# Delta stage: another order of the operations inside a steady slot

## The reference

```python
q = silu(dwconv_causal(x @ Wq, conv_q_w, conv_q_b))     # k and v likewise, 4 taps
alpha = sigmoid(x @ Wa + ba); beta = sigmoid(x @ Wb + bb)
def step(S, inp):                                       # 16 heads, DK = DV = 128, 256 steps
    err = einsum('bhvk,bhk->bhv', S, kt) - vt
    S = at * S - bt * err[..., None] * kt[:, :, None, :]
    return S, einsum('bhvk,bhk->bhv', S, qt)
o = scan(step, S0, (q, k * scale, v, alpha, beta))
o = (o - mean(o)) * rsqrt(var(o) + 1e-05) * ln_w + ln_b # per head
o = (o * sigmoid(x @ Wg)).reshape(B, T, H * DV) @ Wo
```

## Time and profile before

| | |
|---|---|
| median of 3 runs | 3179.25 us (3178.41 to 3184.36) |
| the profiled execution, its own time | 3174.32 us |
| its span, first to last instruction | 3172.5 us |
| PE busy | 2712.6 us, 86% |
| DVE busy | 2251.3 us, 71% |
| ACT busy | 2126.5 us, 67% |
| POOL busy | 2001.5 us, 63% |
| mean granted TensorE clock | 0.943 of full |

### The profile page before, as it was taken

The page is one execution under the profiler, slowest core; times in us unless marked ns, Lnnn a source line. Parts: engine busy times, 40 slices in busy tenths (PEclk is TensorE's granted clock), DMA queues, the critical chain, the costliest instruction groups (busy, mean ns, idle before and its releaser), DMA issues.

```text
span 3172.5 us, 65475 instructions
## 1 busy us (share of the span) xinstructions
PE 2712.6 (86%) x21872; PEld 2201.8 (69%) x21872; DVE 2251.3 (71%) x5574; ACT 2126.5 (67%) x4995; POOL 2001.5 (63%) x2171
## 2 busy tenths in 40 slices
PE   6889889646679999999999999999999999976761
PEld 4555555425568888888888888888888888765651
DVE  5777777575546767767767677677677676688877
ACT  4767776324458778777777777777787787754531
POOL 3544554333766878677786776868768777676432
PEclk9999999667889999999999999999999999988976
DMA  2000000014577676776767767677676767633311
GB/s 98 0 0 0 0 0 0 3 56 126 119 205 193 163 201 156 190 195 160 203 149 192 195 162 197 159 189 191 167 182 173 188 178 176 160 87 88 86 29 53
DMA packets 750313, 402.07 MB, mean 127 GB/s; under 512 B 406867, under 2 KB 686163, under 8 KB 749910
## 3 DMA queue, kind: packets, MB, share of 16 engines
q1 hardware_dynamic: 750038, 398.59, 48.6%
HBM read 263.80 MB, written 134.62 MB: 126 GB/s over the span
## 4 chain that ended last, share of the span: by engine, by line
PE 52%; ACT 6%; DVE 5%; POOL 4%; issue 3%; SPq 0%; DMA 0%; DVEq 0%; POOLq 0%; ACTq 0%
PE bank L2041 22%; PE bank L2092 8%; PE bank L2208 7%; PE bank L2072 4%; PE bank L2156 4%; ACT acc L1116 2%; POOL oT L896 2%; ACT shifted L1114 2%; PE bank L2080 2%; PE bank L2198 1%; PE bank L2126 1%; PE bank L2135 1%; PE bank L2114 1%; ACT oT L1191 1%; ACT TT L1171 1%
## 5 line engine op out<-in xcount | busy, mean ns | idle before, releaser
L863 POOL TENSOR_TENSOR acc<-acc,shifted 128x510 f32<-128x510 f32 x384 | 557.4, 1452 | 455.8 <-DVE acc L1637 455.8
L1637 DVE SCALAR_TENSOR_TENSOR acc<-bank,conv_w,acc 128x254 f32<-128x254 f32 (+1 forms) x1536 | 630.6, 472 | 271.3 <-ACT acc L1116 270.9
L2041 PE MATMUL bank<-x_k,w_kq 128*128 128x256 f32 x2048 | 509.5, 399 | 25.1 <-DMA x_k<-xT_scratch 25.1
L1114 ACT ACTIVATE shifted<-bank,conv_w 128x255 f32<-128x255 f32 x768 | 368.0, 479 | 178.6 <-issue 113.6
L2041 PEld LDWEIGHTS bank<-x_k,w_kq 128*128 128x128 f32 x2048 | 388.5, 197 | 90.2 <-issue 15.2
L1116 ACT ACTIVATE acc<-bank,conv_b,conv_w 128x256 f32<-128x256 f32 x768 | 439.9, 573 | 0.0
L776 POOL TENSOR_TENSOR prob<-prob,rinv 128x512 f32<-128x512 f32 x192 | 202.0, 1055 | 265.9 <-DVE rinv L1433 265.7
L880 POOL TENSOR_TENSOR inv<-inv,outer 128x30 f32<-128x30 f32 (+14 forms) x480 | 287.6, 599 | 37.6
L1660 DVE TENSOR_TENSOR LM<-bank,dec 128x512 f32<-128x512 f32 x256 | 167.7, 687 | 155.7 <-PE bank L2072 146.6
L2208 PE MATMUL bank<-w_o,oT 128*128 128x256 f32 x1024 | 247.3, 386 | 24.5 <-POOL oT L896 23.7
L877 POOL TENSOR_TENSOR outer<-inv 128x30 f32<-128x30 f32 (+14 forms) x480 | 242.7, 506 | 35.6 <-DMA inv<-D_scratch 8.0
(11 more groups left out here) (243 smaller groups left out, 5905.5 us busy)
## 6 DMA issues: line engine op xcount, KB each, us to landing
abc<-decay_scratch SPq DMA_DIRECT2D x64, 512.0 KB, 5.3
MTm<-M_scratch SPq DMA_DIRECT2D x128, 256.0 KB, 3.4
kqm<-q_scratch SPq DMA_DIRECT2D x64, 512.0 KB, 4.6
knm<-k_scratch SPq DMA_DIRECT2D x64, 258.0 KB, 3.2
x_k<-xT_scratch SPq DMA_DIRECT2D x64, 256.0 KB, 2.9
q_scratch<-kq SPq DMA_DIRECT2D x128, 128.0 KB, 2.7
q_scratch<-kq SPq DMA_DIRECT2D x64, 256.0 KB, 3.4
D_scratch<-LM SPq DMA_DIRECT2D x256, 64.0 KB, 2.4
```

Source lines behind the costliest of these rows:

```text
L863: pool.tensor_tensor(dst, dst, shifted[:, u % 2, :, 1:], ALU.add).then_inc(Z["sumk" if u < 4 else "sumv"], 1)
L1114: act.activation(shifted[:, u % 2, i % 2, 1:], pj[:, 0:SEQ - 1], ACT.Copy, scale=conv_w[:, kind, bass.ds(head, 1), TAPS - 2:TAPS - 1].rear ...
L1637: dve.scalar_tensor_tensor(out=acc[:, kind, i, t:], in0=pj[:, 0:SEQ - t], scalar=wcol, in1=acc[:, kind, i, t:], op0=ALU.mult, op1=ALU.add) ...
L2041: mm = pe.matmul(dst[:, i * SEQ:(i + 1) * SEQ], w[:, k, head * DK:(head + 1) * DK], x[:, k, :], start=(k == 0), stop=(k == CT - 1))
```

## The change

In a steady slot the calls are put into another order on ACT, DVE and PE, and the shares of the elimination on POOL are dealt out anew. No operation is added, taken away or altered. The diff:

```diff
 PIECES = 4 * BATCH - 4
-SHARE = (2, 4, 2, 1, 1, 4, 2, 1, 1, 4, 2, 0)
+SHARE = (2, 5, 0, 2, 2, 5, 0, 2, 2, 4, 0, 0)
...
# ScalarE
                     tap(2), joined("x"), tap(3), silu(0)
                     if h is not None:
-                        gate(0), state()
+                        state(), gate(0)
                     tap(4), tap(5)
                     if h is not None:
                         gate(1)
                     silu(1)
                     if n is not None:
-                        affine(0), affine(1)
-                    keys(p), silu(2)
+                        affine(0)
+                    keys(p)
+                    if n is not None:
+                        affine(1)
                     if h is not None:
-                        first_out(), from_state()
-                    values(0), values(1)
+                        from_state()
+                    silu(2), values(0)
+                    if h is not None:
+                        first_out()
+                    values(1)
...
# VectorE
-                    conv(5), decays(p), products(p, 0), products(p, 1), products(p, 2), products(p, 3)
+                    conv(5), decays(p), products(p, 0), products(p, 1), products(p, 2)
                     if h is not None:
                         second_rhs()
+                    products(p, 3)
...
# TensorE
                     join("x"), proj_k(2), proj_k(3)
+                    if middle:
+                        state()
                     if rear:
                         second_out()
                     if middle:
                         proj_g(0)
-                    proj_v(0)
+                    proj_v(0), proj_v(1)
                     if middle:
-                        state()
-                    proj_v(1)
+                        proj_g(1), keys_on_state()
+                    keys(p)
                     if middle:
-                        proj_g(1), keys_on_state(), first_out()
-                    keys(p)
+                        first_out()
+                    if rear:
+                        outT(0)
                     if middle:
                         queries_on_state()
                     if rear:
-                        outT(0), outT(1)
+                        outT(1)
                     products(p, 0), products(p, 1), products(p, 2)
```

## The result

The changed kernel takes 3195.24 us in the median (3191.38 to 3196.47, five runs), the kernel before 3178.84 in the same set. The ratio is 1.0047, with a 95% interval of 1.0034 to 1.0061: slower by 16 us. 3184 was forecast, with a range of its own of 3177 to 3193 for that mechanism and 3164 to 3200 as the range with the rivals; the measured time lies 2 us outside the first and inside the second. The profiled execution took 3195.32 us, 21.0 more than that of before, with a span of 3193.5 us and a mean granted clock of 0.933 (before 0.943). Those two means take in all four parts; between slots 10 and 64 the clock was 0.99 against 1.00 before.

What follows compares the result with a forecast made beforehand. TensorE was taken to bound the steady slots, with waits for ScalarE before second_out and GpSimd before project_out. 3174.3 + 4.5 (steady slots) + 0.5 (filling) = 3179.3 profiled, median about 3184; range 3164 to 3200.

Steps and rivals of the forecast that it cites:

- that mechanism: Steady slots: TensorE's 0.88 us gain is given back through GpSimd's blocked work before gated(0); about +5 us, chance 0.60.
- State ahead of `second_out`: TensorE: four state matmuls fill the idle time before second_out; all behind comes 0.88 sooner, 47.5 us if nothing takes it back.
- GpSimd's chain: GpSimd from ors to gated(0), blocked by VectorE's normalise and scan: slots +0.81 in kind 1, +0.56 kind 2, -0.81 kind 3.
- The far bound of the prediction: Steady slots: if the scan cost GpSimd nothing, gated(0) would come 2.2 us earlier and TensorE's pace would bind; -83 us.
- The race that I could not read from a row: VectorE's scan against GpSimd's column sum in flight: sum assumed to finish first; if GpSimd lost, +12 us.
- Kind 0: Steady slots with the same four columns as before: gated(0) at +26.39 against +26.58, 0.19 us less; -2.5 us over 13 slots.
- a slot's length is the start of `project_out(0)` plus 7.88: Steady slots: the time from project_out(0) to the next solve_cross was taken as 7.88 us.
- The steady sum: The 54 steady slots, all four kinds added: -2.5 + 10.5 + 7.8 - 11.3 = +4.5 us.
- Filling and draining: Pipeline's start and end: one more column in GpSimd's first batch, +0.5 us (-2 to +3); drain 0, within 2.
- GpSimd did not keep up: Steady slots: faster rival said blocks hide behind one another and the 0.88 stays; -83 us, weak form -14; chance 0.17.
- the second rival: Late gated(0) delays add_shifted(5), silu(2) and TensorE's values(0): +12 to +25 us, about 3198; chance 0.20.

Runs made afterwards that it cites:

- the experiment on the state alone: Kernel before with piece 2 empty in all kinds, plus only the state's moves on TensorE and ScalarE: 3102.88 us, ratio 0.9776.
- the short scan: Changed kernel with VectorE's scan in the steady slots cut from 1032 to 8 elements a row: 3096.89 us, ratio 0.9756.
- the order alone: Changed kernel with SHARE put back as in the kernel before, so only the new instruction order: 3163.23 us, ratio 0.9962.
- the 8 matmuls: Changed kernel with 8 unneeded 128x128 matmuls in TensorE's wait ahead of project_out(0), kinds 0 and 1: 3180.23 us, ratio 1.001.

## Why the prediction was right and where it was not

*State ahead of `second_out`.* Right: 47.9 us of waiting gone, and with piece 2 empty the experiment on the state alone shows its two moves to be the whole gain of the order (44 us, 1779.6 against 1735.4).

*GpSimd's chain.* Right in place and size. Expected for kinds 1, 2 and 3 over the steady slots: +10.5, +7.8, -11.3. Measured: +10.6, +7.7, -11.5. The rule that the two engines block each other for a whole instruction gave the ends of `normalise`, scan, `add_shifted(4)` and `gated(0)` in slots 37 to 39 to 0.04 us, and the short scan showed the block as a cause. The far bound of the prediction, a scan that costs GpSimd nothing, was put at -83; the short scan came out at -77 (1731.4 against 1808.4). The race that I could not read from a row (the scan wanting to start while a sum is in flight) went as assumed, as the scan's 2.62 shows.

*Kind 0.* Here the sum was wrong. Expected -2.5; measured +10.3. The start of `project_out(0)` was right, 0.24 a slot earlier than before where 0.19 was forecast (-3.1 in 13 slots). The step that failed is "a slot's length is the start of `project_out(0)` plus 7.88": that held at the full clock only. With a fall it was 9.57 (slot 36). The prediction itself foresaw waits of 2.4 in kind 0 and carried no term for TensorE's clock behind them. Eight falls of 1.68 are 13.4 us, and -3.1 + 13.4 = 10.3.

*The steady sum* was thus +17.0 instead of +4.5.

*Filling and draining.* +3.4 up to slot 10 and +0.6 behind slot 64 were measured in the one pair of profiles, against +0.5 and 0. This neither bears the forecast out nor refutes it. Of the 3.4 some 1.8 arise before the delta stage, in code that is the same. And slot 10 began at 949.0 us in the order alone and at 953.5 in the kernel before, whose filling is the same, and at 952.1 with the 8 matmuls against 956.9 and 957.2 in the changed kernel: the spread between executions is larger than what was to be measured.

*The rivals and the range.* GpSimd did not keep up, nor did its lateness go on into `values(0)`, ahead of which TensorE idled 0.0. The direction (slower, at 0.45 the likeliest) held, but without the falls the steady sum would have grown by 3.6 us only (17.0 - 13.4), too little to tell from none. The time did not lie in the forecast's own range, and it lay in the wide one only because that had been stretched for the second rival, about 3198, which did not occur. So the total was right by luck; what was right by its reasons is the account of kinds 1 to 3. The missing clock term of 13.4 is more than all of the 12.5 us that the steady sum was off.

*What neither kernel had* is the version that the experiments lead to: the state ahead of `second_out` and no column between `powers` and `gated(0)`. It took 3102.88 us, 2.2% under the kernel before; with the whole new order it was 3100.72, 2.3% under the kernel before of that set.

## What to carry to other kernels

A wait that is filled comes back at the next semaphore unless the engine behind that one is also early; so follow, for each kind of slot, how early or late the other engine's chain is, with the time added in which it is blocked by its neighbour. Work that is not urgent should not stand between a late input and an output that TensorE waits for, however small its share. And price a wait of TensorE by more than its length: when a change makes one longer, look at the granted clock behind it. Here a fall cost 1.69 us on top of a wait of 2.35.

## What the runs showed of the hardware that was not expected

- A wait of TensorE of 2.35 us, in steady slots where it waits at most once a slot, was followed by a fall of its clock to half in 8 of 13 cases (the same 8 in a second execution, 11 of 13 in the order alone), at 1.69 us each. Waits of 1.90 us had one behind them in none of 13 slots of the changed kernel and in 5 of 13 of the one with 18 added matmuls; the waits of 1.5 and 1.6 us in these slots never had.
- Eight useless matmuls in that wait, with eight in that of kind 1, won 13.2 us of steady time.
- VectorE's scan over 128x1032 elements blocks GpSimd for its whole length of 2.29 us (`add_shifted(4)` took 3.27 instead of 1.26), and is itself held up by a GpSimd instruction of 0.66 us that began first (2.62 instead of 2.29).
